# Expert 0 takes the first block's two sequences one after the other, and the second sequence's last pieces lie among the first one's expert steps

## The chip, the cores and the metric

The kernel runs on one core of one Trainium2 chip. A core has TensorE (PE in the profile), VectorE (DVE), ScalarE (ACT), GpSimd (POOL) and SyncE (SP, which issues most DMAs). The metric is the device time of one launch in microseconds. The kernel before took 2881.23, 2886.41 and 2884.26 us in three runs, median 2884.26 us.

## The reference

Sixteen sequences of 256 tokens with 256 features go through four residual layers:

```python
x = x + L0(x)   # per sequence: gate, 16 causal scans with their own decay, blend, projection, layer norm
x = x + L1(x)   # per sequence: scores, masked softmax (prefix, postfix or cloze by a type), pooling
# L2: eight gated experts and a shared one, for every token
g = einsum('bsd,edf->ebsf', h, Wg);  u = einsum('bsd,edf->ebsf', h, Wu)
expert_outs = einsum('ebsf,efd->ebsd', silu(g) * u, Wd)
x = x + (1 - sg) * einsum('be,ebsd->bsd', gating_probs, expert_outs) + sg * shared
# L3: one hidden layer of 1024 with gelu, an output of 192 shared and 64 chosen by the sequence's index
x = x + L3(x)
```

## The kernel before

Features lie on the 128 partitions (two halves), tokens along the free axis. Two sequences make a block of 512 tokens, and there are eight blocks.

Two kinds of work run side by side. The *side work* is layers L0 and L1 of one sequence, cut into 47 pieces numbered j = 0 to 46; each of a block's two sequences is a lane (lane 0, lane 1) with its own tiles. Pieces 0 to 6 make the running mean, the gates and the modulation. Pieces 7 to 22 are the 16 scans: PE broadcasts one row (line 620), DVE multiplies two halves (1056) and scans two halves (1064), GpSimd adds the result into `temporal` (1292). Pieces 23 to 46 are the lane's *tail*: projection on PE (539), tanh on ACT (839), product (1072), projection, square (847), variance, square root (856), reciprocal (1081), norm (1084 to 1091), attention score (861, 1095), maximum (1099), exponential (866), probabilities (1113), transposes (659, 668), pooling, and the sum into `acc` (1126).

The *expert work* is one step for each block, each of nine experts and each of eight chunks of 128 hidden units. A step's `front` makes the gate and the up product: 12 matmuls, since every product is made from a high and a low part as three matmuls (546 to 548). ACT takes silu of the gate (915), DVE multiplies with the up product (1158), ACT and GpSimd split the result (943, 1297), and `back` adds the chunk's part of the down product in 6 matmuls. A block's state is split into `res_hi` on ACT (904) and `res_lo` on DVE (1149) before its first step. Weights are split once for each chunk: `w_hi` on ACT (884), `w_lo` on DVE (1134).

The order of everything is one list, made by `order()`; each engine walks through it and issues its own part, so every engine's queue is in that order and waits in order. Block 0 cannot hide its side work behind expert steps, so its pieces come first, by the list `turns0`: lane 1 lies five pieces behind lane 0 and takes turns with it. After its scans stand the `pre` parts, which make two results of layer L0 (`soma`, `mod`) for 14 later sequences while PE is free: 14 units of four parts, with ScalarE functions of its Gelu and Tanh kind. The setup piece `bias` (line 1006 on DVE, 765 on PE) waits for all of them. Only when both lanes have written `acc` does the first front run, for 512 tokens.

ScalarE has to load a table (ACT_TABLE_LOAD in the trace) where the next function isn't in the loaded one: Gelu and Tanh are together, and Sqrt, Exp and Silu are each in another one.

Of the kernel before, what the change touches and what calls it, by code (L numbers as in the profile page):

```python
# [5 lines left out]
P = 128  # L6
# [13 lines left out]

HEAD = NE + 1
# [9 lines left out]
RUNS = []  # L31
for k in range(LAST[-1] + 2):
    if members(k):
        RUNS.append((k % (NE + 1), members(k)))
    RUNS += [(HEAD, [b]) for b in range(NBLK) if k == LAST[b] + 1]

# [13 lines left out]

EARLY = {29: 0, 32: 1, 37: 2, 43: 3}
# [6 lines left out]
for e, blocks in RUNS:  # L58
    first = len(CHUNKS)
    CHUNKS += [(e, blocks[0], c) for c in range(FC)]  # L60
    STEPS += [(e, b, c, first + c) for b in blocks for c in range(FC)]
UPS, CLOSES = [], []
for e, b, c, n in STEPS:
    UPS.append((UPS[-1] if UPS else 0) + (e != HEAD))
    CLOSES.append((CLOSES[-1] if CLOSES else 0) + (c == FC - 1))
# [20 lines left out]
def step_budget(i):  # L86

    return 2.4 if FIRST_USE[STEPS[i][3]] == i else 3.4
# [6 lines left out]
def order():  # L95
# [7 lines left out]
    turns0 = [(0, j) for j in (4, 5, 6, 7)] + [(1, 2), (0, 8), (0, 3), (1, 3), (0, 9), (1, 4), (0, 10), (1, 5), (0, 11), (1, 6)]  # L103
    for j in range(12, PIECES):
        turns0 += [(0, j), (1, j - 5)]
    turns0 += [(1, j) for j in range(PIECES - 5, PIECES)]
    parts = list(PARTS)
    for s, j in turns0:
        out.append(("side", 0, s, j))
        for _ in range((1 if j < 12 and s == 0 else 2) if 7 <= j < 7 + ND else 0):  # L110
            if parts:
                out.append(("pre", *parts.pop(0)))
        if s == 0 and j == 36:
# [13 lines left out]
    for s, n in ((0, PIECES), (1, PIECES)):  # L127
        had[s] += sum(side_cost(b, j) for b, _, j in lanes[s][:n])
        lanes[s] = lanes[s][n:]
    while lanes[0] or lanes[1]:  # L130
# [6 lines left out]
    res = {0: BB}  # L137
# [49 lines left out]
    for r, (e, blocks) in enumerate(RUNS):  # L187
        while res.get(blocks[-1], 0) < BB:
            piece()
        for b in blocks:  # L190
            for c in range(FC):
                kind = "head" if e == HEAD else "experts"
                split_ready(i)
                if (b, kind) not in split:
# [86 lines left out]
def residual_stack_kernel(nc, xT, chunks, head_chunks, sidew, vec128, w64, penalties, ident, we_rows,  # L281
# [6 lines left out]
    with ctx:  # L288
# [163 lines left out]
        def x_at(b):  # L452
            return 16 * (b // 2 + 1)

# [79 lines left out]
        def _(pe):  # L534
# [167 lines left out]
            def front(i):  # L702
                e, b, c, n = STEPS[i]
                k, slot = n % WSLOTS, b % 2
                if i == 0:
                    pe.wait_ge(pre_act, 3 * NPRE)
                if i == FIRST_USE[n]:
                    pe.wait_ge(s_wlo, n + 1)
                if c == 0:
                    pe.wait_ge(s_rlo, SPLIT_AT[b, "head" if e == HEAD else "experts"])  # L710
# [6 lines left out]
                def quads(at_):  # L717
                    cols = [slice(at_ + h * P, at_ + (h + 1) * P) for h in range(DH)]
                    return [(w_hi[k][:, cols[h]], w_lo[k][:, cols[h]], res_hi[slot][:, h, :], res_lo[slot][:, h, :])
                            for h in range(DH)]  # L720

                exact_sum(ps_gate[i % 2][:], quads(0)).then_inc(s_gate, 1)
                if e != HEAD:
                    exact_sum(ps_up[i % 2][:], quads(DH * P)).then_inc(s_up, 1)

            def back(i):
                e, b, c, n = STEPS[i]
                wh, wl = w_hi[n % WSLOTS], w_lo[n % WSLOTS]
# [5 lines left out]
                for h in range(DH):  # L734
                    if h and c == 0 and CLOSES[i]:
                        pe.wait_ge(s_acc, CLOSES[i])
                    if e != HEAD:
                        col = slice(2 * DH * P + h * P, 2 * DH * P + (h + 1) * P)
                        last = exact_sum(ps_out[:, h, :], [(wh[:, col], wl[:, col], hi[:], lo[:])], **ends)
# [28 lines left out]
        def _(act):  # L768
# [127 lines left out]
            def split(slot, b, kind):  # L896
                if kind == "head":
                    act.wait_ge(s_acc, CLOSES[FINAL_EXPERT[b]])
                else:
# [6 lines left out]
            def front(i):  # L906
                e, b, c, n = STEPS[i]
                h = hid[i % 3]
# [5 lines left out]
                else:  # L914
                    activate(h[:], ps_gate[i % 2][:], ACT.Silu).then_inc(s_act, 1)  # L915
# [17 lines left out]
            def late(i):  # L933
                if i == 0:
# [8 lines left out]
                activate(hid_hi[i % DEPTH][:], hid[i % 3][:], ACT.Copy).then_inc(s_hhi, 1)  # L943
# [24 lines left out]
        def _(dve):  # L968
# [177 lines left out]
            def split(slot, b, kind):  # L1146
                dve.wait_ge(s_rhi, split_no[0] + 1)
                split_no[0] += 1
                TT(res_lo[slot][:], acc[b % NACC][:], f(res_hi[slot][:]), ALU.subtract).then_inc(s_rlo, 1)
# [241 lines left out]
```

## Time and profile before

| what | value |
|---|---|
| three runs | 2881.23, 2886.41, 2884.26 us; median 2884.26 |
| the profiled execution | 2885.2 us, span 2883.4 us, mean granted TensorE clock 0.992 |
| PE busy | 2823.0 us, 98% |
| DVE busy | 1844.7 us, 64% |
| ACT busy | 1393.8 us, 48% |
| POOL busy | 1235.9 us, 43% |
| mean DMA traffic | 70 GB/s |

A busy share is the share of the span in which at least one instruction of the engine ran. PE is pipelined: a matmul's record lasts longer than its share of PE's time, so the pace is read from the distance between starts. The granted clock is 1.00 at 2.4 GHz and 0.50 at 1.2 GHz.

### The profile page before, as it was taken

How to read it: one execution, taken by the hardware profiler on the slowest of the kernel's cores; microseconds unless marked ns; L12 is line 12 of the kernel's file. 1: busy time of each engine (PE TensorE's matmuls, PEld its weight loads, DVE VectorE, ACT ScalarE, POOL GpSimd, SP SyncE). 2: the span in 40 equal slices, each digit the busy share in tenths (PEclk: the TensorE clock that was granted, in tenths of full speed). 3: DMA queues.
4: the chain of work that ended last, by engine and by line, in shares of the span. 5: the costliest groups of instructions: out<-in, count | busy, mean ns of one | idle time of the engine just before them, and what ended most of it. 6: DMA issues, size and time to landing. Idle time of an engine off the chain costs nothing.

```text
span 2883.4 us, 36551 instructions
## 1 busy us (share of the span) xinstructions
PE 2823.0 (98%) x13018; PEld 2334.1 (81%) x13018; DVE 1844.7 (64%) x3017; ACT 1393.8 (48%) x2410; POOL 1235.9 (43%) x950
## 2 busy tenths in 40 slices
PE   8699999999999999999999999999999999999998
PEld 5488888788888888888888888888888888888887
DVE  8699778867777766556766666655766563333443
ACT  4544555455336633454534553354643463333554
POOL 5256434643454445433554245542455333333333
PEclk9799999999999999999999999999999999999999
DMA  4143322333112311111211221111221121111231
GB/s 150 50 122 97 92 92 79 112 92 95 58 48 74 116 45 45 48 56 46 91 48 48 61 83 44 48 55 47 84 67 52 48 88 57 44 44 44 70 112 39
DMA packets 85557, 201.22 MB, mean 70 GB/s; under 512 B 10296, under 2 KB 27136, under 8 KB 85376
## 3 DMA queue, kind: packets, MB, share of 16 engines
q1 hardware_dynamic: 82240, 190.38, 21.6%
q0 software_dynamic: 2560, 8.39, 0.9%
q8 instruction: 104, 1.70, 0.2%
q14 instruction: 77, 0.63, 0.1%
q10 hardware_dynamic: 576, 0.11, 0.0%
HBM read 190.75 MB, written 8.09 MB: 69 GB/s over the span
## 4 chain that ended last, share of the span: by engine, by line
PE 88%; DVE 7%; issue 2%; ACT 2%; POOL 1%; DMA 1%; SPq 0%; DVEq 0%; ACTq 0%; POOLq 0%
PE bank L546 19%; PE bank L548 19%; PE bank L547 19%; PE ps_out L546 9%; PE ps_out L548 9%; PE ps_out L547 9%; DVE w_lo L1134 2%; PE bank L539 1%; DVE trace L1064 1%; DVE trace L1056 1%; PE bank L620 1%; DVE hid L1158 0%; PE ps_out L539 0%; DMA stat<-mod_rows 0%; ACT L856 0%
## 5 line engine op out<-in xcount | busy, mean ns | idle before, releaser
L1297 POOL TENSOR_TENSOR hid_lo<-hid,hid_hi 128x512 fp32r<-128x512 f32 x640 | 864.9, 1352 | 1581.4 <-ACT hid_hi L943 1581.0
L546 PE MATMUL bank<-res_lo,w_hi 128*128 128x512 f32 x2432 | 962.3, 396 | 7.6 <-issue 3.5
L548 PE MATMUL bank<-res_hi,w_hi 128*128 128x512 f32 x2432 | 952.5, 392 | 0.0
L547 PE MATMUL bank<-res_hi,w_lo 128*128 128x512 f32 x2432 | 951.5, 391 | 0.0
L1158 DVE TENSOR_TENSOR hid<-hid,bank 128x512 f32<-128x512 f32 x576 | 394.0, 684 | 539.5 <-PE bank L548 510.5
L915 ACT ACTIVATE hid<-bank 128x512 f32<-128x512 f32 x576 | 344.3, 598 | 662.7 <-PE bank L548 662.2
L1134 DVE TENSOR_TENSOR w_lo<-w_raw,w_hi 128x768 fp32r<-128x768 f32 (+2 forms) x520 | 511.5, 985 | 182.5 <-ACT w_hi L884 141.7
L884 ACT ACTIVATE w_hi<-w_raw 128x768 fp32r<-128x768 f32 x392 | 331.5, 846 | 526.9 <-PE ps_out L548 505.7
L548 PEld LDWEIGHTS bank<-res_hi,w_hi 128*128 128x128 f32 x2432 | 458.1, 188 | 103.0
L546 PEld LDWEIGHTS bank<-res_lo,w_hi 128*128 128x128 f32 x2432 | 458.3, 188 | 101.1 <-issue 8.9
L547 PEld LDWEIGHTS bank<-res_hi,w_lo 128*128 128x128 f32 x2432 | 458.7, 189 | 86.4
L546 PE MATMUL ps_out<-hid_lo,w_hi 128*128 128x512 f32 (+1 forms) x1344 | 511.4, 381 | 8.1 <-DVE acc L1181 4.9
L548 PE MATMUL ps_out<-hid_hi,w_hi 128*128 128x512 f32 (+1 forms) x1344 | 510.5, 380 | 0.0
L547 PE MATMUL ps_out<-hid_hi,w_lo 128*128 128x512 f32 (+1 forms) x1344 | 510.3, 380 | 0.0
L943 ACT ACTIVATE hid_hi<-hid 128x512 fp32r<-128x512 f32 x640 | 398.8, 623 | 11.0 <-DVE hid L1158 10.4
L1292 POOL TENSOR_TENSOR temporal<-temporal,trace 128x512 f32<-128x512 f32 x240 | 334.4, 1394 | 31.4 <-DVE trace L1064 31.2
L1064 DVE TENSOR_TENSOR_SCAN trace<-bank,trace 128x256 f32<-128x256 f32 x480 | 304.9, 677 | 8.2
L546 PEld LDWEIGHTS ps_out<-hid_lo,w_hi 128*128 128x128 f32 x1344 | 253.4, 189 | 63.3 <-issue 7.1
L547 PEld LDWEIGHTS ps_out<-hid_hi,w_lo 128*128 128x128 f32 x1344 | 253.4, 189 | 49.5
L548 PEld LDWEIGHTS ps_out<-hid_hi,w_hi 128*128 128x128 f32 x1344 | 253.4, 189 | 47.7
L1056 DVE SCALAR_TENSOR_TENSOR trace<-gated,bl,bank 128x256 f32<-128x256 f32 x512 | 221.6, 474 | 108.4 <-PE bank L620 101.7
L1181 DVE SCALAR_TENSOR_TENSOR acc<-ps_out,coef,acc 128x256 f32<-128x256 f32 x288 | 119.3, 476 | 0.9 <-PE ps_out L548 0.9
(179 smaller groups left out, 1634.8 us busy)
## 6 DMA issues: line engine op xcount, KB each, us to landing
w_raw<-in_chunks SPq DMA_DIRECT2D x392, 384.0 KB, 3.0
w_raw<-in_head_chunks SPq DMA_DIRECT2D x64, 224.0 KB, 2.5
x_in<-in_xT SPq DMA_DIRECT2D x16, 256.0 KB, 3.7
out_yT<-acc SPq DMA_DIRECT2D x8, 512.0 KB, 2.8
pre_x<-in_xT SPq DMA_DIRECT2D x14, 256.0 KB, 7.0
soma_rows<-pre_soma SPq DMA_DIRECT2D x14, 256.0 KB, 2.0
soma<-soma_rows SPq DMA_DIRECT2D x14, 256.0 KB, 3.2
acc<-in_sidew SPq DMA_DIRECT2D x2, 512.0 KB, 7.0
```

Source lines behind the costliest of these rows:

```text
L546: mm(out, wh, xl, start=start and i == 0, stop=False, skip_group_check=not lone)
L547: mm(out, wl, xh, start=False, stop=False, skip_group_check=not lone)
L548: last = mm(out, wh, xh, start=False, stop=end, skip_group_check=not lone)
L884: last = activate(w_hi[k][:], raw[:], ACT.Copy)
L915: activate(h[:], ps_gate[i % 2][:], ACT.Silu).then_inc(s_act, 1)
L943: activate(hid_hi[i % DEPTH][:], hid[i % 3][:], ACT.Copy).then_inc(s_hhi, 1)
L1056: last = STT(tr[:, h, :], gated[s][:, h, :], bl[:, h, d:d + 1], (lead_mix[d % 2] if lead else ps)[:, 0:S], ALU.mult, ALU.mult)
L1064: last = V.tensor_tensor_scan((temporal[s] if d == 0 else tr)[:, h, :], decay.broadcast_to([P, S]), tr[:, h, :], 0.0, ALU.mult, ALU.add)
L1134: return TT(w_lo[k][:, cols], src, f(w_hi[k][:, cols]), ALU.subtract)
L1158: TT(h[:], h[:], ps_up[i % 2][:], ALU.mult).then_inc(s_hid, 1)
L1292: nc.gpsimd.tensor_tensor(temporal[s][:], temporal[s][:], trace[s][d % 3][:], ALU.add).then_inc(l_pool[s], 1)
L1297: nc.gpsimd.tensor_tensor(hid_lo[i % DEPTH][:], hid[i % 3][:], f(hid_hi[i % DEPTH][:]), ALU.subtract).then_inc(s_hlo, 1)
```

## The change

Block 0's first run, expert 0, is cut into two sets of eight steps: the first with lane 0's 256 tokens, the second with lane 1's 256. Every step carries a fifth number (`s`, the lane, or `None` for 512 tokens), and all tiles of such a step are sliced to the lane's columns. The chunks of expert 0's weights are shared by both sets. In `turns0` lane 0 gets ahead of lane 1: lane 0 ends all its 47 pieces when lane 1 has done its last scan (piece 22). Lane 1's 24 tail pieces then lie among lane 0's eight steps: 5, 4, 2, 4, 2, 2, 3 and 2 of them behind the fronts. The first front waits for lane 1's last scan too, because the scans of both lanes use the memory of `ps_up` and `ps_gate`.

```diff
-RUNS = []
-for k in range(LAST[-1] + 2):
+RUNS = [(0, [(0, s) for s in range(BB)])]
+for k in range(1, LAST[-1] + 2):
     if members(k):
-        RUNS.append((k % (NE + 1), members(k)))
+        RUNS.append((k % (NE + 1), [(b, None) for b in members(k)]))
...
+TAIL = [5, 4, 2, 4, 2, 2, 3, 2]
...
-    for j in range(12, PIECES):
-        turns0 += [(0, j), (1, j - 5)]
-    turns0 += [(1, j) for j in range(PIECES - 5, PIECES)]
+    for j in range(15, PIECES):
+        turns0 += [(0, j)] + [(1, k) for k in BESIDE.get(j, ())]
+    tail = [(0, 1, j) for j in range(7 + ND, PIECES)]
...
-        if s == 0 and j == 36:
+        if s == 0 and j == 41:
             while parts:
                 out.append(("pre", *parts.pop(0)))
             out.append(("setup", "bias"))
...
+                if tail:
+                    for _ in range(TAIL[i - 1]):
+                        out.append(("side", *tail.pop(0)))
+                    res[0] = BB if not tail else 1
+                    for n in range(begun, cut):
+                        out.append(("cut_lo", n))
+                    continue
...
                 if i == 0:
                     pe.wait_ge(pre_act, 3 * NPRE)
+
+                    pe.wait_ge(l_dve[1], dve_at(1, 0, f"scan{ND - 1}"))
...
-                exact_sum(ps_gate[i % 2][:], quads(0)).then_inc(s_gate, 1)
+                exact_sum(ps_gate[i % 2][:, tok], quads(0)).then_inc(s_gate, 1)
                 if e != HEAD:
-                    exact_sum(ps_up[i % 2][:], quads(DH * P)).then_inc(s_up, 1)
+                    exact_sum(ps_up[i % 2][:, tok], quads(DH * P)).then_inc(s_up, 1)
...
-                    TT(h[:], h[:], ps_up[i % 2][:], ALU.mult).then_inc(s_hid, 1)
+                    h, tok = hid[i % 3], tokens(STEPS[i][4])
+                    TT(h[:, tok], h[:, tok], ps_up[i % 2][:, tok], ALU.mult).then_inc(s_hid, 1)
...
-                        for s in range(BB):
+                        for s in range(BB) if lane is None else [lane]:
                             q, tok = b * BB + s, slice(s * S, (s + 1) * S)
```

`BESIDE` says which pieces of lane 1 stand behind which piece of lane 0 (`27: (13,)`, `31: (14, 15)`, and so on).

First place, VectorE, where lane 0's scans end. In the kernel before the scans of both lanes take turns, and nothing of a tail is among them (a piece is two multiplies, 1056, and two scans, 1064):

```order
L1056 SCALAR_TENSOR_TENSOR trace_1<-gated,bl,bank 128x256 [waits lane0_pe,lane0_pool]
L1056 SCALAR_TENSOR_TENSOR trace_1<-gated,bl,bank 128x256
L1064 SCALAR_TENSOR_TENSOR trace_1<-bank,trace_1 128x256 [waits lane0_dve]
L1064 SCALAR_TENSOR_TENSOR trace_1<-bank,trace_1 128x256
L1056 SCALAR_TENSOR_TENSOR trace_2<-gated,bl,bank 128x256 [waits lane1_pe,lane1_pool]
L1056 SCALAR_TENSOR_TENSOR trace_2<-gated,bl,bank 128x256
L1064 SCALAR_TENSOR_TENSOR trace_2<-bank,trace_2 128x256 [waits lane1_dve]
L1064 SCALAR_TENSOR_TENSOR trace_2<-bank,trace_2 128x256
```

In the changed kernel this is VectorE from the maximum of lane 0's scores on (1084 and 1092 are the lines of 1056 and 1064):

```order
L1127 TENSOR_REDUCE top<-trace_0 128x2 [waits lane0_dve]
L1129 TENSOR_SCALAR top<-top 128x2 [waits lane0_dve]
L1031 TENSOR_TENSOR side_lo<-acc,side_hi 128x1024 [waits setup_act]
L1084 SCALAR_TENSOR_TENSOR trace_0<-gated,bl,bank 128x256 [waits lane1_pe,lane1_pool]
L1084 SCALAR_TENSOR_TENSOR trace_0<-gated,bl,bank 128x256
L1092 SCALAR_TENSOR_TENSOR trace_0<-bank,trace_0 128x256 [waits lane1_dve]
L1092 SCALAR_TENSOR_TENSOR trace_0<-bank,trace_0 128x256
L1034 TENSOR_SCALAR bias_b<-ps_out,v 128x16 [waits setup_pe]
L1084 SCALAR_TENSOR_TENSOR trace_1<-gated,bl,bank 128x256 [waits lane1_pe,lane1_pool]
L1084 SCALAR_TENSOR_TENSOR trace_1<-gated,bl,bank 128x256
```

Lane 1's scans now stand behind instructions that wait for lane 0's tail, for ScalarE's weight splits (`setup_act`) and for the bias (`setup_pe`).

Second place, ScalarE in the changed kernel, from lane 0's exponential to the copy of its transposed probabilities. The `pre` parts (953, 958) now reach into the tail:

```order
L888 ACT_TABLE_LOAD
L888 ACTIVATE trace_1,den<-trace_0,top 128x256 [waits lane0_dve]
L888 ACTIVATE trace_1,den<-trace_0,top 128x256
L892 ACT_TABLE_LOAD
L892 ACTIVATE junk<-eps 128x1
L894 ACTIVATE gated<-bank 128x512 [waits lane0_pe]
L953 ACT_TABLE_LOAD [waits pre_out1]
L953 ACTIVATE pre_soma_60<-ps_out,v 128x256 [waits pre_pe]
L953 ACTIVATE pre_soma_60<-ps_out,v 128x256
L958 ACTIVATE pre_mod_65<-bank,bn_half 16x256 [waits pre_pe]
L906 ACTIVATE w_hi<-w_raw 128x768 [waits raw_in0]
L897 ACTIVATE soma<-bank 128x512 [waits lane0_pe]
```

In the kernel before, the same stretch has no `pre` part; all of them are ahead of lane 0's tail:

```order
L866 ACT_TABLE_LOAD
L866 ACTIVATE trace_1,den<-trace_0,top 128x256 [waits lane0_dve]
L866 ACTIVATE trace_1,den<-trace_0,top 128x256
L870 ACT_TABLE_LOAD
L870 ACTIVATE junk<-eps 128x1
L872 ACTIVATE gated<-bank 128x512 [waits lane0_pe]
L884 ACTIVATE w_hi<-w_raw 128x768 [waits raw_in0]
L861 ACTIVATE small<-bank,c 64x256 [waits lane1_pe]
L875 ACTIVATE soma<-bank 128x512 [waits lane0_pe]
```

So three of the table loads are between kinds of work that before never met.

Third place, TensorE in the changed kernel, behind the second front (the last row is the third front's first matmul):

```order
L567 MATMUL bank<-res_hi,w_lo 128x256
L568 MATMUL bank<-res_hi,w_hi 128x256
L559 MATMUL bank<-trace_0,acc 128x256 [waits setup_pool,lane1_act,lane1_dve]
L559 MATMUL bank<-trace_0,acc 128x256 x3
L566 MATMUL bank<-res_lo,w_hi 128x256 [waits hidden,w_lo]
L567 MATMUL bank<-res_hi,w_lo 128x256
L568 MATMUL bank<-res_hi,w_hi 128x256
```

In the kernel before, the second front is followed by the third at once. Its first front (the last two rows here) has lane 1's whole tail ahead of it:

```order
L659 MATMUL bank<-idn,temporal 128x128 x3
L668 MATMUL bank<-idn,trace_1 128x128 [waits lane1_act,lane1_dve]
L668 MATMUL bank<-idn,trace_1 128x128 x3
L539 MATMUL bank<-soma,gated 128x256 [waits lane1_act]
L539 MATMUL bank<-soma,gated 128x256 x3
L546 MATMUL bank<-res_lo,w_hi 128x512 [waits res_lo,w_lo,pre_act]
L547 MATMUL bank<-res_hi,w_lo 128x512
```

The fronts of lane 0 now stand in one queue with the tail of lane 1, and each waits behind the other.

## Rows read from the trace of the kernel before

**Rows 1.** The page: busy shares, and the granted clock in 40 slices.

```profile
PE 2823.0 (98%) x13018; PEld 2334.1 (81%) x13018; DVE 1844.7 (64%) x3017; ACT 1393.8 (48%) x2410; POOL 1235.9 (43%) x950
...
PEclk9799999999999999999999999999999999999999
```

**Rows 2.** Stretches: start:end, us; busy us of each engine (instructions); clock, DMA share, GB/s.

```profile
22.00:92.00 70.00, 64.37 (x246) 41.60 (x245) 65.37 (x126) 27.47 (x63) 38.56 (x31) 0.92 0.25 87
92.00:130.00 38.00, 21.26 (x79) 15.58 (x77) 21.07 (x34) 25.59 (x39) 1.49 (x2) 0.81 0.16 49
...
75.00:80.00 5.00, 4.65 (x11) 3.57 (x12) 3.94 (x8) 0.62 (x2) 3.99 (x4) 0.50 0.01 2
...
150.00:155.00 5.00, 5.00 (x23) 3.87 (x21) 4.97 (x8) 2.52 (x5) 1.98 (x2) 1.00 0.27 79
155.00:160.00 5.00, 4.55 (x22) 3.72 (x21) 4.96 (x9) 1.11 (x2) 0.00 (x0) 1.00 0.30 82
160.00:165.00 5.00, 4.91 (x23) 3.76 (x22) 4.97 (x8) 3.56 (x7) 2.60 (x3) 1.00 0.76 232
```

**Rows 3.** TensorE in order of time: start, us, line, tiles, form; idle before in brackets.

```profile
75.35 0.58 PE L620 MATMUL bank<-mod_pair,sel 128*128 128x256 f32 x1 [2.13 <-DVE trace L1056]
75.72 3.62 PE L539 MATMUL ps_out<-pre_x,acc 128*128 128x256 f32 x8
...
124.60 1.99 PE L539 MATMUL bank<-soma,gated 128*128 128x256 f32 x8 [0.69 <-ACT soma L875]
129.88 0.77 PE L546 MATMUL bank<-res_lo,w_hi 128*128 128x512 f32 x1 [3.28 <-DVE res_lo L1149]
...
136.48 0.39 PE L547 MATMUL bank<-res_hi,w_lo 128*128 128x512 f32 x1
...
140.79 0.39 PE L548 MATMUL bank<-res_hi,w_hi 128*128 128x512 f32 x1
143.66 0.39 PE L546 MATMUL bank<-one_lo,side_hi 128*128 128x256 f32 x1 [2.48 <-DVE two_lo L1031]
143.88 0.28 PE L547 MATMUL bank<-one_hi,side_lo 128*128 128x256 f32 x1
...
146.48 0.29 PE L548 MATMUL bank<-two_hi,side_hi 128*128 128x256 f32 x1
```

**Rows 4.** VectorE's scans in order of time.

```profile
16.68 0.87 DVE L1056 SCALAR_TENSOR_TENSOR trace<-gated,bl,bank 128x256 f32<-128x256 f32 x2
...
22.05 0.87 DVE L1056 SCALAR_TENSOR_TENSOR trace<-gated,bl,bank 128x256 f32<-128x256 f32 x2 [1.13 <-PE bank L620]
...
60.83 1.27 DVE L1064 TENSOR_TENSOR_SCAN trace<-bank,trace 128x256 f32<-128x256 f32 x2
...
62.90 1.27 DVE L1064 TENSOR_TENSOR_SCAN trace<-bank,trace 128x256 f32<-128x256 f32 x2
...
89.54 1.27 DVE L1064 TENSOR_TENSOR_SCAN trace<-bank,trace 128x256 f32<-128x256 f32 x2
```

**Rows 5.** VectorE in the tails, in order of time.

```profile
98.47 0.96 DVE L1134 TENSOR_TENSOR w_lo<-w_raw,w_hi 128x768 fp32r<-128x768 f32 x1 [5.14 <-ACT w_hi L884]
...
102.42 1.75 DVE L1081 RECIPROCAL stat<-stat 128x256 f32<-128x256 f32 x1 [1.09 <-ACT stat L856]
104.20 0.69 DVE L1084 TENSOR_TENSOR ema<-ema,stat 128x512 f32<-128x512 f32 x1
...
112.31 1.22 DVE L1003 TENSOR_TENSOR side_lo<-acc,side_hi 128x1024 fp32r<-128x1024 f32 x1
...
126.63 0.69 DVE L1126 TENSOR_TENSOR acc<-bank,temporal 128x512 f32<-128x512 f32 x1 [3.43 <-PE bank L539]
```

**Rows 6.** ScalarE's table loads and kinds of work in the tails, and one `pre_soma`.

```profile
85.78 0.84 ACT L926 ACTIVATE pre_soma<-ps_out,v 128x256 f32<-128x256 f32 x2 [2.68 <-PE ps_out L539]
...
98.46 1.28 ACT L839 ACT_TABLE_LOAD   x1
99.76 0.84 ACT L839 ACTIVATE trace<-bank,half 128x256 f32<-128x256 f32 x2
```

More of the change, by code:

```diff
@@ L59 @@
     first = len(CHUNKS)
-    CHUNKS += [(e, blocks[0], c) for c in range(FC)]
-    STEPS += [(e, b, c, first + c) for b in blocks for c in range(FC)]
+    CHUNKS += [(e, blocks[0][0], c) for c in range(FC)]
+    STEPS += [(e, b, c, first + c, s) for b, s in blocks for c in range(FC)]
 UPS, CLOSES = [], []
-for e, b, c, n in STEPS:
+for e, b, c, n, s in STEPS:
     UPS.append((UPS[-1] if UPS else 0) + (e != HEAD))
@@ L86, in step_budget @@
 def step_budget(i):
+    if STEPS[i][4] is not None:
+        return 1.0
     return 2.4 if FIRST_USE[STEPS[i][3]] == i else 3.4
@@ L109, in order @@
         out.append(("side", 0, s, j))
-        for _ in range((1 if j < 12 and s == 0 else 2) if 7 <= j < 7 + ND else 0):
+        for _ in range((2 if s or j >= 12 else 1) if 7 <= j < 7 + ND else 0):
             if parts:
                 out.append(("pre", *parts.pop(0)))
-        if s == 0 and j == 36:
+        if s == 0 and j == 41:
             while parts:
@@ L129, in order @@
         lanes[s] = lanes[s][n:]
+    out.append(("split", 0, 0, "lane0"))
     while lanes[0] or lanes[1]:
@@ L187, in order @@
     for r, (e, blocks) in enumerate(RUNS):
-        while res.get(blocks[-1], 0) < BB:
+        while r and res.get(blocks[-1][0], 0) < BB:
             piece()
-        for b in blocks:
+        for b, s in blocks:
             for c in range(FC):
-                kind = "head" if e == HEAD else "experts"
+                kind = "head" if e == HEAD else "lane0" if s == 0 else "experts"
                 split_ready(i)
-                if (b, kind) not in split:
+                if kind != "lane0" and (b, kind) not in split:
                     if queue:
@@ L453, in x_at, with tokens @@
             return 16 * (b // 2 + 1)
+        def tokens(s):
+            return slice(0, BT) if s is None else slice(s * S, (s + 1) * S)
         x_blk = xT.rearrange("(h p) t -> p h t", p=P)
@@ L738, in back @@
                         col = slice(2 * DH * P + h * P, 2 * DH * P + (h + 1) * P)
-                        last = exact_sum(ps_out[:, h, :], [(wh[:, col], wl[:, col], hi[:], lo[:])], **ends)
+                        last = exact_sum(ps_out[:, h, on], [(wh[:, col], wl[:, col], hi[:, on], lo[:, on])], **ends)
                     elif h == 0:
@@ L898, in split @@
                     act.wait_ge(s_acc, CLOSES[FINAL_EXPERT[b]])
+                elif b == 0:
+                    s = 0 if kind == "lane0" else 1
+                    act.wait_ge(l_dve[s], dve_at(s, b, "res"))
+                    activate(res_hi[0][:, :, tokens(s)], acc[0][:, :, tokens(s)], ACT.Copy).then_inc(s_rhi, 1)
+                    return
                 else:
@@ L933, in late @@
             def late(i):
+                tok = tokens(STEPS[i][4])
                 if i == 0:
@@ L1148, in split @@
                 split_no[0] += 1
+                if b == 0 and kind != "head":
+                    tok = tokens(0 if kind == "lane0" else 1)
+                    TT(res_lo[0][:, :, tok], acc[0][:, :, tok], f(res_hi[0][:, :, tok]), ALU.subtract).then_inc(s_rlo, 1)
+                    return
                 TT(res_lo[slot][:], acc[b % NACC][:], f(res_hi[slot][:]), ALU.subtract).then_inc(s_rlo, 1)
```

35 lines of the change are left out of this document (19 added, 16 removed).

## The prediction

> **What bounds the kernel now.** I read the page first: TensorE is busy in 98% of the span and its clock is full in nearly every slice, with the first slice at 0.7 and 0.9 [rows 1]. Nothing but TensorE's total work and the places where it doesn't work can move the end. The stretches say where: from 22 to 92 us VectorE is the busy one (65.4 of 70 us) and TensorE fills itself with early parts; from 92 to 130 us no engine is over 26 of 38 us busy, TensorE has 21.3 at a mean clock of 0.81, so this is latency, the two tails; behind 150 us TensorE is busy 14.46 of 15 us [rows 2]. The change touches only what lies ahead of that. From block 3 on, the two orders are the same list with eight added to the step numbers, so what is won or lost at the start is kept to the end.
>
> The measure I use is a virtual start: the time at which TensorE could have begun the expert work and then run without a gap. In the kernel before the first front starts at 129.88 us, at half clock, there is an idle 2.48 us, and from 143.66 us TensorE runs through [rows 3]. Until there it has done two fronts, 24 matmuls of 512 columns. One takes (140.79 - 136.48) / 19 = 0.227 us at full clock [rows 3], together 5.4 us; 143.66 - 5.4 is 138.2 us, and with the 0.5 us of idle time after 150 [rows 2] it is **138.8 us**.
>
> **Width.** 256 columns at full clock take (146.48 - 143.88) / 22 = 0.118 us [rows 3], two of them 0.237 against 0.227. Expert 0 has 8 x 18 matmuls, each now cut in two: 144 x 0.0106 = 1.5 us more, all of it on the path.
>
> **Until lane 0's last scan.** Lane 0 ends its scans with the 21st piece of the two lanes. In the kernel before the 21st piece's scans start at 62.90 and last 1.27 us [rows 4], end 64.2. The wait of 1.13 us at 22.05 [rows 4] goes, since lane 1's eight soma matmuls no longer stand ahead of that broadcast: 63.0 us.
>
> **Until lane 1's last scan.** VectorE has 11 pieces of lane 1 left, 2.07 us each (60.83 to 62.90) [rows 4], 22.8 us, and lane 0's tail between them. That tail by the distances between starts: four weight splits at 0.9, reciprocal 1.75, norm of three steps 2.1, a side weight split 1.15, product, scores, maximum, probabilities, sum and bias 0.6 + 0.65 + 0.8 + 0.9 + 0.7 + 0.2 [rows 5]; together 12.4 us. Without a wait the last scan would end at 63.0 + 22.8 + 12.4 = 98.2 us, against 90.8 now (89.54 + 1.27) [rows 4]. But VectorE takes its queue in order, and these instructions wait for others. I walked through the queue with these durations: lane 1's piece 13 waits for a broadcast that stands behind lane 0's projection (1.8 us), piece 14 likewise (1.1), a weight split for ScalarE (1.8), five small ones together 2.0. Then the bias. It needs the last `pre` part, and on ScalarE this now stands behind lane 0's exponential: load 1.28, two exponentials 1.1, load 1.28, a one-column silu 0.2, copy 0.5, load 1.28, `pre_soma` 0.84, `pre_mod` 0.45, in all 6.9 us from 93.0 [rows 6]. TensorE's bias matmul and VectorE's add follow at 100.4, while VectorE would have got there at 95.2: 5.2 us. The waits sum to 11.9, the last scan ends at 110.1, and with the state's split (0.6 us for half the size) the first front starts at **110.9 us**, 19.0 earlier than now.
>
> This is with TensorE at full clock. The trace shows that an idle stretch as short as 2.13 us is followed by 1.2 GHz: eight matmul records take 3.62 us from 75.72 on, and the clock is 0.50 from 75 to 80 us [rows 2, 3]. In lane 0's tail TensorE waits about 3 us for the norm, and the same walk with the lower clock behind it gives 113.7. I take the middle, 112.3.
>
> **Lane 1's tail among the steps.** Bare, from the last scan to the split state, the chain is: GpSimd add 1.3, projection 2.0 (four matmuls, eight records, 1.99 us) [rows 3], tanh 0.8, product 0.6, projection at the lower clock 3.3, two copies 1.1, variance 1.0, load and square root 1.75, reciprocal 1.7, norm 2.1, attention 1.1, tanh 0.5, score 0.9, add 0.7, maximum 0.8, exponential 1.1, probabilities 0.9, transposes 0.7, copy 0.6, pooling 2.0, sum 0.7, split 1.3: 27.0 us. What the steps put ahead of its links, again by the queues: the projection behind front 0, both at the low clock after an idle 3 us, 3.6; the product behind the second step's multiply and ScalarE's side weight split 3.8; the reciprocal behind a silu table load, the silu, two splits and a third side weight split 4.3; attention at the low clock 1.4; the maximum behind step 5's multiply 1.6; the probabilities behind a table load and step 6's silu 2.7; the pooling behind front 7 and a back 1.5; small ones 0.5. Together 19.4. So front 8, lane 1's first, starts at 110.1 + 27.0 + 19.4 + 0.1 = 156.6, and 1.4 later by the clock term above: **158.0 us**. Its bounds: 137 + 2 without any of these waits, and 168 with a low clock throughout (third rival).
>
> By then TensorE has done eight fronts and five backs of lane 0, 126 matmuls of 0.118, 15.0 us. So the new virtual start is 158.0 - 15.0 + 1.5 (width) = 144.5, and I add 1.0 for a restart at the low clock after the idle 2 us ahead of front 8 (a front at half clock is 1.4 us longer; bounds 0 to 3). 145.5 - 138.8 = 6.7 us later.
>
> What else moves is hidden: GpSimd and VectorE have halved instructions in 16 steps; the eight silus, splits and weight cuts of these steps lie in the walk above. One more addition into `acc` comes in the second set (two multiply-adds of 0.45 us); TensorE has a front of 1.4 us ahead of the matmuls that wait for it. Block 1's side work starts up to five steps later, and it is needed only 64 full steps on. SP's loads are ahead of use by three chunks as before.
>
> **Table loads, by row and rule.** From lane 0's projection to lane 1's last silu reload the order has 13 table loads, nine before. A load's record is 1.28 us, and the activation behind it starts at 99.76 where the load ends at 99.74 [rows 6]: nothing is added, and the walk counts 1.28 each. The Trainium skill, "ScalarE: Activation LUTs", section "What ACT_TABLE_LOAD costs", puts a drain of some 1.38 us to each load; the trace disagrees by its 0.02 us. By that rule the four extra loads would make 5.5 us more.
>
> **The sum.** The profiled execution took 2885.2 us (span 2883.4 and 1.8 around it): 2885.2 + 6.7 = 2891.9. It lies 0.9 above the median of the runs, so I predict **2891 us**.
>
> **The rivals.**
> - *The tail keeps its pace* (0.25). In the kernel before the way from lane 1's last scan (90.8) to the first front (129.88) was 39 us with another lane in all queues [rows 3, 4]; my 46 may charge waits that overlap. Then front 8 starts at 111.5 + 39 = 150.5, the virtual start is 138.0: 0.8 us faster, 2883.5. If the bias wait is hidden as well, 5.2 more: 2878, faster. It decides at front 8 before 151.3 us. For it: VectorE has only 21.1 of 38 us to do in the tails [rows 2]. Against it: the waits come from order, not from load.
> - *The low clock stays* (0.12). TensorE has some 27 us of work in 46, in pieces with waits between them. If it stays at 1.2 GHz throughout, the tail's matmuls not yet charged (some 6 us at full clock) and the four fronts ahead of its links (5.7 us) double, less a part in waits: 10 us, front 8 at 168, 2901. The mean clock of 0.81 in the old tails [rows 2] speaks against all of it.
> - *VectorE's backlog behind front 8* (0.10). Lane 1's steps are 2.1 us on TensorE, and from step 11 VectorE has one weight split of 0.9, a multiply of 0.4 and a third of a piece for each, some 2.4: five steps would lose up to 4 us, 2895.
> - *A table load costs a second time its length* (0.03): four more loads of 1.28, 2896; rows 6 speak against it.
>
> The forecast itself has 0.45, with its own range 2885 to 2897 (front 8 between 152 and 164); the rest, 0.05, is open to both sides.
>
> **Chances.** A measurement here tells 0.2% or 5.8 us from nothing. Slower by more: 0.27 of the forecast (its border is front 8 at 157), and the second to fourth rival: 0.52. Within: 0.17 of the forecast, 0.13 of the first rival, a little of the rest: 0.31. Faster: 0.17, from the first rival. The range that leaves out 2 in 10 is 2878 to 2901.
>
> **What would show it.** First front near 112 us, front 8 near 158; a VectorE wait of about 5 us ahead of the bias near 95 us; 13 loads in that stretch; 256-column matmuls 0.118 us apart where they run full; TensorE idle behind the second front and ahead of the attention for over 3 us each. I'm wrong if the first front comes before 106 us, if front 8 comes before 151, or if TensorE waits again between 165 and 200 us.

## The result, and the profile after

The changed kernel takes 2901.97 us (median; 2901.01 to 2905.97, a disturbed run left out), the kernel before 2884.02 beside it: ratio 1.0069, 95% interval 1.0055 to 1.0082. It is slower by 18 us; 2891 was forecast, with a range up to 2901. The profiled execution took 2901.01 us (span 2899.2), 15.8 more than that of before. In a second set it took 2902.99 (2897.79 to 2905.74) beside 2882.28, ratio 1.0064 (1.0051 to 1.0077). By the medians the two kernels are 18 to 21 us apart.

The page of the changed kernel, the lines that answer to [rows 1]; then its stretches, which answer to [rows 2] (start:end, length, busy us of TensorE, weight load, VectorE, ScalarE, GpSimd with instructions, granted clock, DMA):

```profile
PE 2824.9 (97%) x13162; PEld 2344.9 (81%) x13162; DVE 1841.6 (64%) x3026; ACT 1399.7 (48%) x2431; POOL 1240.8 (43%) x958
...
PEclk9799999999999999999999999999999999999999
```

```profile
92.00:130.00 38.00, 21.53 (x90) 17.54 (x91) 19.04 (x33) 17.85 (x33) 7.82 (x8) 0.78 0.17 53
130.00:160.00 30.00, 19.28 (x115) 17.18 (x115) 13.23 (x24) 14.85 (x27) 6.26 (x8) 0.83 0.21 63
160.00:170.00 10.00, 10.00 (x85) 10.00 (x86) 6.46 (x14) 4.65 (x11) 5.09 (x6) 1.00 0.28 92
```

Where before had one stretch of 38 us with TensorE idle for 17, now there are two, 68 us with 27 idle, at a mean clock of about 0.8. From front 8 on TensorE is nearly full: it is idle for 2.1 us up to step 72, 312 us later. In order of time, VectorE's bias and lane 1's last scan, and ScalarE's first table load behind 92 us ([rows 4, 6]):

```profile
101.39 0.23 DVE L1034 TENSOR_SCALAR bias_b<-ps_out,v 128x16 f32<-128x16 f32 x1 [5.00 <-PE ps_out L787]
...
112.77 1.27 DVE L1092 TENSOR_TENSOR_SCAN trace<-bank,trace 128x256 f32<-128x256 f32 x2
```

```profile
93.76 1.28 ACT L888 ACT_TABLE_LOAD   x1
95.06 0.51 ACT L888 ACTIVATE trace<-trace,top 128x256 f32<-128x256 f32 x1
```

And TensorE, with its idle time in brackets ([rows 3]):

```profile
114.77 0.55 PE L566 MATMUL bank<-res_lo,w_hi 128*128 128x256 f32 x1 [3.42 <-DVE res_lo L1179]
...
124.48 3.64 PE L559 MATMUL bank<-trace,acc 128*128 128x256 f32 x8 [3.62 <-DVE trace L1100]
...
140.50 2.08 PE L559 MATMUL bank<-temporal,wa 128*128 128x256 f32 x4 [5.76 <-DVE temporal L1119]
...
159.84 0.38 PE L566 MATMUL bank<-res_lo,w_hi 128*128 128x256 f32 x1 [2.17 <-DVE res_lo L1179]
```

The walk is there: the bias wait is 5.0 us (forecast 5.2), front 0 at 114.77 (112.3), waits over 3 us behind the second front and ahead of the attention, front 8 at 159.84 (158.0). ScalarE has 13 table loads between 72.45 and 149.87, as forecast. So the mechanism held. What is missing lies elsewhere, and to find them I compared the start of every expert step in two traces, step n of before with the step of the same chunk after. The difference is 11.9 us at step 72, 11.2 at 90 and at 150, 12.8 at 180, 14.4 at 200 and 15.8 from 400 to the end. In between, from 72 on, the difference stays the same to within 0.1 us.

### The profile page after: what moved, and what is told of

Same layout as the page of the kernel before. It is cut to its first block, busy times and chain, and to the rows that moved or that the text cites. A ratio compares the mean times of both kernels' runs of the same rounds, so it can differ in the third digit from the quotient of the medians.

```text
span 2899.2 us, 36904 instructions
## 1 busy us (share of the span) xinstructions
PE 2824.9 (97%) x13162; PEld 2344.9 (81%) x13162; DVE 1841.6 (64%) x3026; ACT 1399.7 (48%) x2431; POOL 1240.8 (43%) x958
## 4 chain that ended last, share of the span: by engine, by line
PE 88%; DVE 6%; ACT 3%; issue 2%; POOL 1%; DMA 1%; SPq 0%; DVEq 0%; ACTq 0%; POOLq 0%
PE bank L566 19%; PE bank L568 19%; PE bank L567 19%; PE ps_out L566 9%; PE ps_out L568 9%; PE ps_out L567 9%; PE bank L559 2%; DVE w_lo L1162 2%; DVE trace L1092 1%; DVE trace L1084 1%; PE bank L640 1%; DVE hid L1190 0%; DMA stat<-mod_rows 0%; PE bank L688 0%; ACT w_hi L906 0%
## 5 line engine op out<-in xcount | busy, mean ns | idle before, releaser
L1330 POOL TENSOR_TENSOR hid_lo<-hid,hid_hi 128x512 fp32r<-128x512 f32 (+1 forms) x648 | 866.4, 1337 | 1569.1 <-ACT hid_hi L971 1568.5
L566 PE MATMUL bank<-res_lo,w_hi 128*128 128x512 f32 (+1 forms) x2464 | 970.6, 394 | 10.0 <-DVE res_lo L1179 5.6
L568 PE MATMUL bank<-res_hi,w_hi 128*128 128x512 f32 (+1 forms) x2464 | 959.4, 389 | 0.0
L567 PE MATMUL bank<-res_hi,w_lo 128*128 128x512 f32 (+1 forms) x2464 | 958.7, 389 | 0.0
L1190 DVE TENSOR_TENSOR hid<-hid,bank 128x512 f32<-128x512 f32 (+1 forms) x584 | 394.8, 676 | 555.0 <-PE bank L568 523.9
L942 ACT ACTIVATE hid<-bank 128x512 f32<-128x512 f32 (+1 forms) x584 | 345.6, 592 | 670.0 <-PE bank L568 668.5
L566 PEld LDWEIGHTS bank<-res_lo,w_hi 128*128 128x128 f32 x2464 | 465.8, 189 | 103.1 <-issue 8.9
L568 PEld LDWEIGHTS bank<-res_hi,w_hi 128*128 128x128 f32 x2464 | 465.7, 189 | 101.5
L567 PEld LDWEIGHTS bank<-res_hi,w_lo 128*128 128x128 f32 x2464 | 466.4, 189 | 85.2
L971 ACT ACTIVATE hid_hi<-hid 128x512 fp32r<-128x512 f32 (+1 forms) x648 | 400.4, 618 | 12.7 <-DVE hid L1190 12.2
L566 PEld LDWEIGHTS ps_out<-hid_lo,w_hi 128*128 128x128 f32 x1360 | 256.5, 189 | 62.9 <-issue 7.2
```

Source lines behind the costliest of these rows:

```text
L566: mm(out, wh, xl, start=start and i == 0, stop=False, skip_group_check=not lone)
L567: mm(out, wl, xh, start=False, stop=False, skip_group_check=not lone)
L568: last = mm(out, wh, xh, start=False, stop=end, skip_group_check=not lone)
L942: activate(h[:, tok], ps_gate[i % 2][:, tok], ACT.Silu).then_inc(s_act, 1)
L971: activate(hid_hi[i % DEPTH][:, tok], hid[i % 3][:, tok], ACT.Copy).then_inc(s_hhi, 1)
L1190: TT(h[:, tok], h[:, tok], ps_up[i % 2][:, tok], ALU.mult).then_inc(s_hid, 1)
```

## The experiments

"Start" below is the difference of step 24's start from the first trace of before, negative is earlier; it is +9.5 for the changed kernel. It is a number of one execution: two traces of the kernel before differ in it by 4.3 us, as shown further down, so a difference of 4 us or less between two single traces says little about the kernels.

**e1, the turns only.** The new `turns0` and `BESIDE`, lane 1's tail whole ahead of front 0, steps of 512 tokens.

> The new turn order of the two lanes alone: lane 0 gets ahead, then lane 1's whole tail, and only then expert 0 with 512 tokens as before. Theory (queue waits): lane 1's last scan ends at 114 us as in the changed kernel, its bare tail of 27 us and a few weight splits follow, so the first front starts near 144 us, 14 later than before, and the time is 2884 + 14 = 2898 us; the steps among the tail then gave back only what they cost. Rival (the halves cost it): the turns alone are near 2887 us. Rival (the clock behind 400 us costs it): the start up to step 30 is later by some 14 us here too, and the rest is low-clock windows of 1.6 us each.

Measured: 2903.61 (2901.85 to 2904.68) beside 2882.56, ratio 1.0077 (1.0063 to 1.0091). TensorE's front 0:

```profile
149.04 0.67 PE L549 MATMUL bank<-res_lo,w_hi 128*128 128x512 f32 x1 [3.29 <-DVE res_lo L1152]
```

That is 19.2 us later than before, start +18.8. Lane 1's last scan starts at 113.53, 0.8 later than in the changed kernel, and ends at 114.80; the tail behind it takes 34.2 us though no step stands between its links. The theory had 27 us and front 0 near 144. One reason shows in TensorE's rows, where three products of the tail run at half clock, 3.75 to 3.78 us instead of 1.99. One of them:

```profile
121.65 3.76 PE L542 MATMUL bank<-trace,acc 128*128 128x256 f32 x8 [1.66 <-DVE trace L1075]
```

The turns alone cost the whole difference. Halving expert 0's steps and laying the tail among them gains and costs nothing that the times show: 2903.61 here, 2901.97 and 2902.99 with it.

**e2, the halves only.** Half steps for expert 0, but the old turns and both tails ahead of front 0.

```
-    tail = [(0, 1, j) for j in range(7 + ND, PIECES)]
+    tail = []
...                    # turns0 as in the kernel before
-    res = {0: 1}
+    res = {0: BB}
```

> Expert 0 in two sets of eight half steps alone, with the kernel before's turn order and both tails ahead of it. Theory (queue waits): only the width is paid, 288 matmuls at 0.1198 against 144 at 0.2268 us, 1.8 us, and ScalarE's and VectorE's first steps are shorter, so 2884 to 2888 us. Rival (half steps starve TensorE: VectorE's weight splits cannot keep up with 2.1 us steps): 2893 us or more, with TensorE idle in the second set.

Measured: 2879.07 (2877.28 to 2884.22), ratio 0.9993 (0.9984 to 1.0002); front 0 at 125.34, start -5.7. The half steps do not make the kernel slower. Their width should cost 1.8 us (288 x 0.1198 against 144 x 0.227); against it, TensorE waits 1.47 us for the smaller split ahead of front 0 and goes on at full clock, where before waits 3.28 us and starts at half clock. Of the 5.7 us, 4.3 are also the difference between before's own two traces.

**e3, the bias late.** The bias stands behind lane 1's last scan, on all engines.

```
-            out.append(("setup", "bias"))     # behind the last `pre` part
...
+    out.append(("setup", "bias"))             # ahead of lane 0's split
...                                            # and its place in SETUP_DVE
```

> The changed kernel with the bias piece moved behind lane 1's last scan. Theory (queue waits): the 5.0 us VectorE wait at 96 to 101 us goes, lane 1's last scan ends near 109 instead of 114 us, everything behind it is 5 earlier: 2897 us. Rival (slack): VectorE waits for ScalarE's chain of table loads at the next instruction, the probabilities, and front 8 stays within 1.5 us of 159.8: 2901 us.

Measured: 2896.75 (2891.34 to 2898.59), ratio 1.0049 (1.0035 to 1.0062). In its trace front 0 is at 110.73, 4.0 us earlier than in the changed kernel, front 8 at 157.52, 2.3 earlier, and 2.5 are left at the end. The last scan moved from 112.77 to 108.59; of the wait of 5.0 us some 4 come back at front 0 and 2 at front 8. But this execution was the slowest of its five (2898.59): the median is 5.2 to 6.2 us under the changed kernel's, which is what the theory said (2897). Whether the tail swallows part of the gain stays open.

**e4 and e5, the tail ahead of steps, and the late parts.** e4 is e3 with more of lane 1's tail ahead of fronts 3, 5 and 6; e5 is e4 with two splits of the side work's weights, `part1` and `part2`, behind fronts 8 and 9 instead of 1 and 3.

```
-TAIL = [5, 4, 2, 4, 2, 2, 3, 2]
+TAIL = [5, 4, 6, 0, 3, 3, 1, 2]     # e4 and e5
...
-                if i in (2, 4):      # from here on e5 alone
-                    out.append(("setup", f"part{i // 2}"))
+                if i in (9, 10):     # i is one more than the front just made
+                    out.append(("setup", f"part{i - 8}"))
```

> The version with the bias late, and more of sequence 1's tail put ahead of fronts 2 and 4 (5, 4, 6, 0, 3, 3, 1, 2 instead of 5, 4, 2, 4, 2, 2, 3, 2 pieces behind fronts 0 to 7); the cutting of the steps' work stays where it is. e5_parts_late did this and also moved lane 0's early parts, and won 9.8 us over e3_bias_late. Theory (the tail's links waited behind fronts and silus that need not be ahead of them): most of it, 6 to 9 us, comes from the tail's place: front 8 near 150, 2889. Rival (the parts were it): 2 us or less of it, front 8 near 156, 2895.

> The kernel with the late bias, and in lane 1's tail the chain put ahead of the steps: pieces 34 to 37 stand right behind 33, pieces 40 to 43 ahead of the next step's multiply, and the two side weight splits part1 and part2 behind front 8. Theory (queue waits): the product 2.4, the reciprocal 4.3, the maximum 1.6 and the probabilities 1.5 us earlier, together 9 to 10 beside the 5 of the bias: front 8 near 146 us and 2888 us. Rival (the chain itself, not its neighbours, is the time): front 8 near 154 us, 2896 us.

Measured: e4 2889.13 (2884.94 to 2892.90), ratio 1.0023 (1.0014 to 1.0032), front 8 at 149.92; e5 2886.98 (2883.55 to 2889.92), 1.0015 (1.0006 to 1.0024), front 8 at 148.03. The one line of numbers is worth 7.6 us between e3 and e4, with the same work on every engine: waits by order, not by load. The late parts add 2.2. TensorE in e5, where the waits of 3.62 and 5.76 us of the changed kernel are 1.44 and 1.96:

```profile
120.95 1.99 PE L559 MATMUL bank<-trace,acc 128*128 128x256 f32 x8 [1.44 <-DVE trace L1100]
...
131.51 2.06 PE L559 MATMUL bank<-temporal,wa 128*128 128x256 f32 x4 [1.96 <-DVE temporal L1119]
...
148.03 0.39 PE L566 MATMUL bank<-res_lo,w_hi 128*128 128x256 f32 x1 [2.17 <-DVE res_lo L1179]
```

**e6, the last three pieces.** e2 with lane 0's state split right behind lane 0's tail, and lane 1's pieces 44 to 46 behind fronts 0 and 1 (`TAIL = [2, 1]`).

> The version with halves, the old turns and both tails ahead, but sequence 0's state is split as soon as sequence 0's tail is through, so fronts 0 and 1 need not wait for sequence 1's last pieces; those (44 and 45, then 46) lie behind fronts 0 and 1. Theory (work in halves pays only where the steps wait for little of the other lane): front 0 starts 2 to 4 us earlier than in e2_halves_only, front 8 follows fronts 0 to 7 without a gap, and the time is 2 to 4 us less, near 2876 beside a 2882.5 of the kernel before. Rival (VectorE's queue holds the last pieces back behind the steps' own work): front 0 comes earlier and front 8 waits as much, the time is that of e2_halves_only, 2879.

Measured: 2879.69 (2875.62 to 2885.25), ratio 0.9990 (0.9981 to 0.9998). Its trace starts 3.0 us earlier than e2's (start -8.7, front 0 at 121.19), the median shows nothing of it. Theory and rival can't be told apart by the times: both kernels' runs spread over 7 to 10 us.

**e8, side work earlier.** The changed kernel, but its steps 16 to 35 are given 0.5 us more side work each in `step_budget`.

> The changed kernel, but steps 16 to 35 are given 0.5 us more side work each, so that block 1's side pieces lie again within a step or so of where the kernel before has them. Theory (of the 5 us that come behind front 8, 1.7 to 2.4 arise between steps 37 and 62, where the changed kernel does these pieces up to five steps later and bunched, and TensorE waits for VectorE): the difference to before at the start of a step stays near 9.5 to 10 from step 16 to step 62 instead of growing to 11.8, and the time is 1.2 to 2.4 us less than that of the changed kernel. Rival (the growth comes of low-clock stretches that fall there by chance): the difference grows as in the changed kernel or at other steps, no change in time.

Measured: 2901.91 (2899.87 to 2902.66), ratio 1.0065 (1.0052 to 1.0078). The theory fell. The difference to before grows by 1.4 us from step 16 to step 90, against 1.9 in the changed kernel: side matmuls that are moved across a step move its start, and are no loss. A loss is only TensorE's idle time. From front 8 to step 72 it is 2.1 us in the changed kernel, all of it between steps 37 and 62, and 2.0 in e8, where 1.7 of it lie at two waits around 222 and 236 us: the waits moved with the work and did not go.

**Both kernels a second time.** The changed one as it is, and the one before.

> The changed kernel itself, for a second trace. Theory (between the start and the end only low-clock stretches differ from one execution to another, 1.6 us each): starts of steps 8 to 36 differ from the first trace by under 0.3 us, the low-clock stretches behind step 62 fall at other steps or in another number, and the whole time differs from 2901.0 by about 1.6 us times the difference in their number. Rival (the three late stretches belong to the new order): they fall at steps 167, 184 and 348 again.

> The kernel before itself, for a second trace. Theory (every execution gets its own low-clock stretches at the start, 1.6 us each on the path): front 0 within 1.7 us of 129.88, the steps behind it at the same distances, and the difference in whole time explained by the low-clock stretches alone. Rival (something other than the clock moves whole executions): distances of steps differ where the clock is full.

Measured: the changed kernel's second trace (2904.22 us) stands 3.4 us behind its first at step 24 and 3.2 at the end, before's second (2880.49) 4.3 ahead of its first at step 24 and 4.4 at step 620. In both pairs an execution has nearly its whole difference by 165 us. Both theories missed by this: they allowed 0.3 us between steps 8 and 36 and 1.7 us at front 0. For the kernel before the trace shows where it comes from. TensorE waits 2.13 us at 75.35 in the first trace and 2.12 in the second; in the first the eight records behind it take 3.62 us, at half clock [rows 3], in the second 1.89, and by 87 us, at the next long wait, the second is 4.3 us ahead:

```profile
74.92 0.38 PE L620 MATMUL bank<-mod_pair,sel 128*128 128x256 f32 x1 [2.12 <-DVE trace L1056]
75.14 1.89 PE L539 MATMUL ps_out<-pre_x,acc 128*128 128x256 f32 x8
```

The stretches of the second trace of the changed kernel:

```profile
92.00:130.00 38.00, 21.89 (x80) 16.47 (x79) 18.94 (x33) 16.85 (x29) 7.99 (x7) 0.68 0.17 52
130.00:160.00 30.00, 21.00 (x125) 19.32 (x124) 12.20 (x22) 16.18 (x30) 5.43 (x7) 0.81 0.16 51
```

The clock is 0.68 where the first had 0.78, front 0 comes at 116.50 and front 8 at 163.21. And the late low stretches fell again at the same steps as in the first trace, which was the rival's. What they are, TensorE's rows show, of the changed kernel's first trace and then of before's at the same step:

```profile
892.16 0.38 PE L640 MATMUL bank<-mod_pair,sel 128*128 128x256 f32 x1 [1.88 <-DVE trace L1092]
892.39 0.58 PE L566 MATMUL bank<-res_lo,w_hi 128*128 128x512 f32 x1
892.76 0.63 PE L567 MATMUL bank<-res_hi,w_lo 128*128 128x512 f32 x1
893.19 0.63 PE L568 MATMUL bank<-res_hi,w_hi 128*128 128x512 f32 x1
```

```profile
880.94 0.38 PE L620 MATMUL bank<-mod_pair,sel 128*128 128x256 f32 x1 [1.88 <-DVE trace L1064]
881.16 0.39 PE L546 MATMUL bank<-res_lo,w_hi 128*128 128x512 f32 x1
881.39 0.40 PE L547 MATMUL bank<-res_hi,w_lo 128*128 128x512 f32 x1
881.62 0.40 PE L548 MATMUL bank<-res_hi,w_hi 128*128 128x512 f32 x1
```

The same wait of 1.88 us; behind it one runs eight matmuls at 0.43 us, half clock, and the other stays at 0.23. That costs 1.6 us, three times in the changed kernel (at 892, 967 and 1681 us) and not in before. So the idle time alone does not say what follows: in the two traces of each kernel waits of 1.88 to 3.03 us are followed by the one clock or the other (2.48 us ahead of 143.66 in before and 2.17 ahead of front 8 in the changed kernel by the full one), and those of 3.15 us and more, from the tails on, by the half one.

**e9, e10, e11, the clock.** Matmuls on constants (256 columns, no one reads them) fill TensorE's waits: in the changed kernel (e9), before (e10) and e6 (e11).

```
+    for _ in range(WARM.get(place, 0)):
+        mm(to[:, 0:S], wsoma[2][:, 0, 0:P], wsoma[2][:, 1, 0:S], start=True, stop=True)
```

> The changed kernel with matmuls on constants (256 columns, results unused) put into TensorE's queue ahead of nine waits of the start: 4, 12, 18, 15 and 12 of them in lane 0's tail, ahead of the bias and ahead of front 0, 13, 22, 8 and 8 in lane 1's tail and ahead of front 8; at 0.24 us each they fill most of each wait, so that the clock should not fall. Theory (the low clock lengthens links of both tails: trace product 3.64 instead of 1.99, score product 2.08 instead of 1.13, the pooling of lane 0 3.47 instead of 1.99, fronts 0 and 4 by 1.4 and 1.7, small ones 1.5; together 8 us of which some lie beside other work): front 8 at 152 to 155 instead of 159.8, the time 5 to 8 us less than that of the changed kernel, near 2896. Rival (the clock costs the 2.4 us that the prediction gave it, the rest is waits by order): 2899.5.

> The kernel before with the same filling ahead of its six waits between 88 and 130 us (11, 12, 7, 20, 6 and 12 matmuls). Theory (there the low clock lengthens two projections by 1.6 and 1.3 us, one score product by 0.95 and the first 14 matmuls of the steps by 0.2 each, 2.8): front 0 2 to 4 us earlier, and 5 to 6 us less in all, 2877. If it and e9_warm gain alike, the 18 to 20 us between the two orders aren't the clock's. Rival (the low clock is what makes the new order slow): e9_warm gains 8 or more, this one under 3.

> e6_last_three with the filling ahead of its five longest waits (11, 10, 11, 19 and 8 matmuls). Theory: what it gains over e6_last_three is its low-clock links, two of 1.0, two of 0.9 and 0.8: 3 us, 2876 to 2877, below the kernel before by 0.2%. Rival (the matmuls without use delay the links behind them as much as the clock does): no gain, 2880.

Measured: 2903.94, 2889.49 and 2881.86; ratios 1.0071 (1.0057 to 1.0085), 1.0022 (1.0013 to 1.0031), 1.0000 (0.9991 to 1.0009). A miss of mine: a matmul in float32 stands as two records of 0.22 us, as the projections show (four in the code, eight in [rows 3]), so the fillings were twice as long as the waits and delayed the links. The clock was 1.00 in e9 from 92 to 170 us, yet front 8 came at 166.33. With half as many:

> e9_warm with half as many filling matmuls (2, 6, 9, 8 and 6 up to front 0, 7, 12, 4 and 4 up to front 8), now 0.44 us each by its trace, so that each filling is about as long as the wait it stands in, or a little shorter. Theory (the low clock costs the changed kernel 5 to 8 us at its start): front 0 at 112 to 114, front 8 at 153 to 156, 2895 to 2897. Rival (it costs no more than the 2.4 us of the prediction): front 8 at 158, 2899.5 or more.

> e10_before_warm with half as many (6, 6, 3, 10, 3 and 6). Theory: front 0 at 124 to 126, with the steps behind it at full clock 2.8 us more; step 8 is 4 to 6 us earlier than in the kernel before's first trace and near that of its second, 2878. Rival (the filling delays the links as much as the clock does): no gain, 2882.

> e11_six_warm with half as many (6, 5, 6, 9 and 4). Theory: front 0 at 118 to 120 instead of 124.12 (full fillings) and 121.19 (none), 2875 to 2877, faster than the kernel before by 0.2%. Rival: as e6_last_three, 2879 to 2880.

Measured: e9b 2888.23 (2886.05 to 2890.40), ratio 1.0022 (1.0013 to 1.0031); e10b 2876.97 (2873.50 to 2879.75), 0.9979 (0.9970 to 0.9988); e11b 2873.60 (2870.48 to 2881.63), 0.9974 (0.9965 to 0.9983). TensorE in e9b (L587 is the filling), and its stretches:

```profile
110.69 0.36 PE L566 MATMUL bank<-res_lo,w_hi 128*128 128x256 f32 x1 [0.84 <-DVE res_lo L1191]
...
115.35 3.19 PE L587 MATMUL bank<-acc 128*128 128x256 f32 x14
119.13 1.99 PE L559 MATMUL bank<-trace,acc 128*128 128x256 f32 x8 [0.59 <-DVE trace L1112]
...
127.58 5.34 PE L587 MATMUL bank<-acc 128*128 128x256 f32 x24
133.50 1.13 PE L559 MATMUL bank<-temporal,wa 128*128 128x256 f32 x4 [0.57 <-DVE temporal L1131]
...
150.28 0.38 PE L566 MATMUL bank<-res_lo,w_hi 128*128 128x256 f32 x1 [0.44 <-DVE res_lo L1191]
```

```profile
92.00:130.00 38.00, 34.83 (x192) 29.88 (x191) 21.18 (x37) 23.04 (x39) 9.34 (x10) 1.00 0.18 57
130.00:160.00 30.00, 27.22 (x187) 24.71 (x186) 16.47 (x33) 12.45 (x28) 9.37 (x12) 1.00 0.27 80
```

Work that nobody needs makes the changed kernel 14 us faster and the kernel before 6; e10's rival had said 8 or more and under 3. The links that ran at half clock in the changed kernel, 3.64 and 2.08 us, take 1.99 and 1.13. Front 8 comes 9.6 us earlier than in the changed kernel's first trace, 12.9 than in its second. With the fillings the new order still is 11.3 us slower than the old (2888.23 against 2876.97; 12.4 by the two ratios), of some 20 without them (2902.5 against 2882.7; 19 by the ratios). Each of these medians is known to 3 or 4 us, and the fillings differ in number and place and may delay a link themselves, so this division is rough.

**e12, both.** e5 with the fillings (2, 6, 8, 6 up to front 0, then 3, 4 and 4).

> e5_parts_late with filling matmuls ahead of seven waits (2, 6, 8 and 6 up to front 0, 3, 4 and 4 up to front 8). Theory (the two gains add: the waits by order 15 us, the clock 10 to 14 of which some lie in waits that are gone): front 0 near 108, front 8 near 142, the time 2877 to 2880, between the kernel before and e11b_six_warm_half at 2873.6. Rival (with the waits gone the fillings only delay, and the clock is worth under 3 us): 2884 to 2887.

Measured: 2878.88 (2874.25 to 2881.77), ratio 0.9983 (0.9974 to 0.9992); front 8 at 139.38, start -9.5. TensorE's stretch, the clock full:

```profile
92.00:130.00 38.00, 33.96 (x196) 28.55 (x195) 27.08 (x46) 24.68 (x44) 11.98 (x11) 1.00 0.23 74
```

The gains add in part: against the changed kernel e5 gains 15.5 us, e9b 14.3, and both together 23.6. With fillings in all of them, the turns at their best (e12, 2878.88) are not ahead of the old order (e10b, 2876.97). The fastest version is e11b: by the medians 9.2 us under before, by the ratio 7.5. Some 6 of it is the filling, which the kernel before gains as well; its trace starts 12.9 us earlier.

## Why the prediction was wrong

The direction and the mechanism were right, and the marks of the walk came within 2.5 us in the first trace; the time was 9 us short in the profiled execution (2891.9 against 2901.0) and 11 in the median, 1 us past the upper end of the range. No single term makes that up. Its steps in turn:

- **The step that failed first: "Until there it has done two fronts, 24 matmuls of 512 columns."** It is three. TensorE's rows of the kernel before, each the first of a front:

```profile
129.88 0.77 PE L546 MATMUL bank<-res_lo,w_hi 128*128 128x512 f32 x1 [3.28 <-DVE res_lo L1149]
...
135.14 0.63 PE L546 MATMUL bank<-res_lo,w_hi 128*128 128x512 f32 x1
...
138.29 0.39 PE L546 MATMUL bank<-res_lo,w_hi 128*128 128x512 f32 x1
```

 36 matmuls are 8.2 us, not 5.4; the virtual start was 136.0 and not 138.8. This is 2.7 us, and a count along the rows would have found it. Alone it is more than what the range was missed by.
- **Front 8** was 1.8 us late, the pace 0.1198 instead of 0.118 (0.3), TensorE's idle time in block 1's side work grew by 1.3 (2.1 us behind front 8, where before has 0.8 beyond the 0.5 already counted); the restart at low clock behind front 8 (1.0) didn't come. With the miscount: 6.7 + 2.7 + 1.8 + 0.3 + 1.3 - 1.0 = 11.8, and 11.9 is measured at step 72.
- **"What is won or lost at the start is kept to the end"** failed as well, by 4.0 us in these traces. By step 90 before's own low stretch at 520 us gives 0.6 back, and the late low stretches at the same waits of 1.9 and 2.1 us add 4.6. They aren't the new order's: e10b, which has the old one, has them at the same steps (its difference goes from -6.9 at step 90 to -2.7 at 400), and e4, which has the new one, has none of them (4.8 and 4.7). Which executions get them stays open; with them the 15.8 are complete.
- **The low clock was sized at 1.4 + 1.0 us.** At full clock front 0 comes at 110.69, where the walk without the low clock said 110.9. In the changed kernel it came at 114.77 and 116.50: 4.1 and 5.8 us for the clock, not 1.4. From there to front 8 the walk's 45.7 us held (45.1) only since it contained low-clock prices (3.6, 1.4 and 3.3 us); at full clock it is 39.6. Its two parts were off against each other, and that their sum held is partly luck: the bare tail, 27.0 us in the walk, took 34.2 in e1, and the steps added 11.6 (45.8 from the last scan's end to front 8) and not 19.4. The second rival, which gave 2901 for a clock that stays low throughout, had the nearest time, but by luck: front 8 came at 160 and not at 168, and the mean clock was 0.8 and not 0.5.
- **The base.** The profiled execution of before lay 2.4 to 2.9 us above the medians of the 15 to 29 runs taken beside the experiments (2882.3 to 2882.8): it has the half clock behind the wait at 75.35, which the second trace has not. The prediction took off only 0.9. So the medians are 18 to 21 us apart where the traces are 15.8.
- **A slip of the sum:** 110.1 and 0.6 for the split are 110.7, not 110.9.
- **Right:** the width (1.5 us; 1.8 by the measured pace), the bias wait (5.0), lane 0's last scan (63.0 forecast; it ends at 62.9), no backlog of VectorE behind front 8, and the 13 table loads at 1.28 us each. The Trainium skill, "ScalarE: Activation LUTs", section "What ACT_TABLE_LOAD costs", puts a drain of some 1.38 us to each load. The trace does not agree: the activation starts 0.02 us behind the end of the load at 93.76, and the load at 112.64 starts 0.02 us behind the activation ahead of it:

```profile
111.99 0.63 ACT L924 ACTIVATE res_hi<-acc 128x512 fp32r<-128x512 f32 x1 [4.29 <-DVE acc L1154]
112.64 1.28 ACT L942 ACT_TABLE_LOAD   x1
```

In one sentence: the turns put two tails one behind the other, which costs some 11 to 12 us with TensorE kept at full clock, and the waits in them lower its clock, which costs the new order some 7 to 8 us more than the old.

## What to carry to other kernels

A wait on an engine whose clock follows its work can be paid twice: once as time, and once in the matmuls behind it (3.64 us here instead of 1.99), which may be the next link of the same chain. In a latency-bound stretch price the waits above 3 us with the half clock behind them, put the shorter ones down as uncertain (1.88 to 3.03 us went either way here), or fill them with matmuls that no one reads, a little shorter in all than the wait (fillings twice as long were 8 to 16 us slower here than the right ones). Putting one chain among another's steps moves the waits and doesn't remove them: ask of each link what stands ahead of it in each queue, and move the link first (one line of numbers gave 7.6 us here). And before a sum rests on one trace, count the rows it rests on, and take a second trace to see how far executions differ: 3.4 and 4.3 us here, more than most terms of the sum.

## What was not expected of the hardware

- The same idle time of 1.88 us is followed by half clock in one execution and not in another; where it is, the matmuls behind it take 0.43 us instead of 0.23, and 1.6 us are lost. It recurred at the same steps in both traces of the changed kernel, and in e10b, which has the old order.
- Filling raised the granted clock of the changed kernel's span from 0.991 to 0.998 and took 0.5% off its time, without a change in what the kernel computes.
- A float32 matmul of 256 columns stands as two records, 0.22 us apart; the filled stretches run at 0.44 us for each in the code.
